# Cross attention on one core: three rotating units of two PSUM banks, one side bank, and a new order of the side work

## The reference, cut to what matters

```python
q = _split_heads(queries @ w_q.T + b_q)          # queries: layernorm(x); 16 heads of 16
k = _split_heads(keys @ w_k.T + b_k)             # keys, values: the context, 4096 rows
v = _split_heads(values @ w_v.T + b_v)
scores = einsum('bhqd,bhkd->bhqk', q, k) / sqrt(16)
weights = softmax(scores, axis=-1)
out = merge(einsum('bhqk,bhkd->bhqd', weights, v)) @ w_o.T + b_o
x = x + out
```

## Time and profile before

| of the profiled execution | |
|---|---|
| first cross attention (L862 to the last L134) | 0 to 1048 us |
| its first max matmul, its first scores | 40.0 and 80.5 us |
| second cross attention | 2961 to 3996 us |
| busy in 100 to 950 us: PE, DVE, ACT | 92%, 75%, 66% |
| granted PE clock in 100 to 950 us | 0.99 of full speed |
| busy DMA engines in the same stretch | 57% |

### The profile page before, as it was taken

One profiled execution on the slowest core, in us unless ns is written; L12 is line 12 of the kernel. 1 busy time (PEld: TensorE's weight loads), 2 busy tenths in 40 slices (PEclk: granted clock), 3 DMA queues, 4 the chain that ended last, 5 costly groups with the idle time before them and its releaser, 6 DMA issues. The chain is left out here.

```text
span 4469.0 us, 83297 instructions
## 1 busy us (share of the span) xinstructions
PE 4072.7 (91%) x30320; PEld 2916.0 (65%) x30320; DVE 3121.6 (70%) x7923; ACT 2814.7 (63%) x5769; POOL 1809.5 (40%) x1862
## 2 busy tenths in 40 slices
PE   6899999898979999999999999968999999977898
PEld 4555555555757888888878888845555555545677
DVE  5677777776777767667677676546777777767645
ACT  3666666667976777777677676715666666654322
POOL 3322222212566565555556555413223222201544
PEclk8999999999989999999999999989999999988999
DMA  6655556545020100001100101036556555512265
GB/s 153 133 105 108 103 98 115 109 64 203 10 76 5 34 31 30 24 29 32 39 22 25 38 22 38 15 84 138 114 101 111 102 106 106 100 27 70 83 177 190
DMA packets 208206, 354.14 MB, mean 79 GB/s; under 512 B 26927, under 2 KB 110564, under 8 KB 205745
## 3 DMA queue, kind: packets, MB, share of 16 engines
q1 hardware_dynamic: 200217, 338.42, 34.0%
q0 software_dynamic: 7584, 10.39, 0.7%
HBM read 257.48 MB, written 114.98 MB: 83 GB/s over the span
## 5 line engine op out<-in xcount | busy, mean ns | idle before, releaser
L754 DVE TENSOR_REDUCE xa_m_part<-xa_ring 128x1 f32<-128x512 f32 x2048 | 1318.4, 685 | 501.6 <-PE xa_ring L907 487.1
L676 ACT ACTIVATE xa_ex<-xa_sc 128x1024 f32<-128x1024 f32 x1024 | 991.4, 1022 | 120.6 <-PE xa_sc L893 105.4
L907 PE MATMUL xa_ring<-xa_ks,xa_q_base 48*128 48x512 f32 x2048 | 521.4, 500 | 166.9 <-DVE xa_m_part L754 131.6
L921 PE MATMUL xa_pv<-xa_ex,xa_vs 128*17 128x256 f32 x8192 | 553.1, 388 | 1.7 <-issue 1.7
L1068 POOL TENSOR_SCALAR lt_p<-lt_p,lt_stat 128x192 f32<-128x192 f32 x384 | 354.6, 924 | 456.0 <-DVE lt_stat L1058 455.4
L907 PEld LDWEIGHTS xa_ring<-xa_ks,xa_q_base 48*128 48x128 f32 x2048 | 202.6, 186 | 497.5 <-DVE xa_m_part L754 431.0
L1911 PE MATMUL lt_bank<-lt_wp,lt_xt 128*128 128x512 f32 x1728 | 465.6, 411 | 13.6 <-DVE lt_wp L1748 6.0
L893 PE MATMUL xa_sc<-xa_q_base,xa_ks 50*128 50x256 f32 x4096 | 423.7, 302 | 27.9 <-ACT xa_k L648 4.5
L893 PEld LDWEIGHTS xa_sc<-xa_q_base,xa_ks 50*128 50x128 f32 x4096 | 347.7, 188 | 122.3 <-ACT xa_vs L663 24.6
L1078 ACT ACTIVATE lt_p<-lt_p,lt_stat 128x128 f32<-128x128 f32 (+1 forms) x768 | 321.8, 420 | 157.4 <-DVE lt_stat L1053 154.8
L1911 PEld LDWEIGHTS lt_bank<-lt_wp,lt_xt 128*128 128x128 f32 x1728 | 315.2, 192 | 78.7 <-DVE lt_xt L1741 9.1
(11 more groups left out here) (325 smaller groups left out, 7943.0 us busy)
## 6 DMA issues: line engine op xcount, KB each, us to landing
xa_ks<-keys SPq DMA_DIRECT2D x372, 256.0 KB
keys<-xa_kp SPq DMA_DIRECT2D x128, 512.0 KB, 3.8
xa_cx<-in_ctx_t SPq DMA_DIRECT2D x64, 512.0 KB
lt_u<-in_lt_wqkv SPq DMA_DIRECT2D x54, 256.0 KB
places<-in_moe_blank SPq DMA_DIRECT2D x47, 258.0 KB, 9.6
moe_xs<-places SPq DMA_DIRECT2D x47, 258.0 KB
lt_w<-in_lt_w SPq DMA_DIRECT2D x6, 1536.0 KB
xa_q_base<-xa_m_rows SPq DMA_DIRECT2D x512, 2.0 KB
```

The costliest lines, as they stand in the source:

```text
L676: act.activation(x.ex[:, n % x.NE, :, :], x.sc[n % 2][:, :, :], ACT.Exp).then_inc(*x.ex_done.one())
L754: dve.tensor_reduce(x.m_part[:, i % 2, qt, h, ch:ch + 1], x.bank(n + odd), AX.X, ALU.max).then_inc(*x.dve_out.one())
L907: pe.matmul(x.bank(n + odd), x.q_base[rows, pair, b * S + qt * P:b * S + (qt + 1) * P], x.ks[unit % x.NU][rows, pair % 4, ch * 512:(ch + 1 ...
L921: mm = pe.matmul(x.pv[32 * j:32 * j + x.VW, :], x.vs[:, i % x.NV, kt, 4 * g + j, :], x.ex[:, n % x.NE, 2 * (j % 2) + j // 2, :], start=(kt ...
```

## The change

It touches `Cross` alone, in both stages.

- Banks: seven banks are dealt out anew. `units` are three tensors of two banks each, `pv` is one bank and `side` one. Max and scores of successive slots take turns in the three units: scores, max, scores, max, each the next unit. A step waits until the step three before it has been reduced (DVE) or exponentiated (ACT).
- Side work goes to `side` once weighing has begun, and to `side` and `pv` in turn before that. A `gather` that stands right behind a `max_rows` uses the other half of the same bank, with one common wait on ACT.
- The two heads of a max are reduced by one DVE instruction of 128 x (2 x 512), with one semaphore increment, in place of two of 128 x 512.
- The order in a step of two slots is now: scores, max, weigh, weigh, scores, max, then side work. `max_rows` and `gather` come together at the start of each quad (`gather` half a quad later than before).
- A key, value or query comes in each step whose side place is free (two in each step of the lead). `may_fill` holds back values until their buffer is free. In an item that gives side work in eight steps, `max_rows` with `gather` in four, and none in four. turn_out and project_out now take such places too, four slots later than before.
- The queries of batches 1 to 3, and their `stack_q`, move from slots 10 to 42 into the lead. `stack_k` is requested at slots 0 and 16 of an item, two slots earlier; that of unit 1 stands apart.
- `combine` is cut into three parts (L784; L786; the rest), in three successive steps.
- A memset of `xa_pv` (L716) goes.

```diff
-            self.ring = [ps(f"ring{i}", [P, 512]) for i in range(self.NW)]
-            self.pv = ps("pv", [P, S])
-            self.sc = [ps(f"sc{i}", [P, 4, S]) for i in range(2)]
+            self.units = [ps(f"unit{i}", [P, 2, 512]) for i in range(self.UNITS)]
+            self.pv, self.side = ps("pv", [P, 512]), ps("side", [P, 512])
...
+        queries = lambda b: [("query", b, mt) for mt in range(2)]
+        first = values(0)
+        out = self.keys(0, 1) + first[0:2] + queries(1) + first[2:4] + queries(2) + queries(3)
...
-        jobs = iter(self.filling())
-        for t in range(-self.LEAD, total + 20, 2):
+        jobs = self.filling()
+        outputs = [(batch * (b + 1) + at, (kind, b)) for b in range(B)
+                   for at, kind in ((18, "turn_out"), (22, "project_out"))]
+        for t in range(-self.LEAD, total + 24, 2):
             top = t + self.LEAD
             quad, at = divmod(t, 8)
             side = []
             if at == 0 and 0 <= quad + 1 < 4 * self.ITEMS:
                 side.append(("max_rows", quad + 1))
-            if at == 4 and 1 <= quad <= 4 * self.ITEMS:
-                side.append(("gather", quad - 1))
-            if t < 0 or at % 4 == 0:
-                job = next(jobs, None)
-                if job is not None:
-                    side.append(job)
-                    if job[0] == "value" and job[2] % 2 == 1:
-                        m = 2 * (job[1] + 1) + job[2] // 2
-                        if m < 2 * self.ITEMS:
-                            side.append(("split", m))
-                        if m + 2 < 2 * self.ITEMS:
-                            side.append(("ctx", m + 2))
-            b, at_b = divmod(t - 10, 12)
-            if 0 <= b < B - 1 and at_b in (0, 4):
-                side.append(("query", b + 1, at_b // 4))
-            if 0 <= b < B - 1 and at_b == 8:
-                side.append(("stack_q", b + 1))
-            b, at_b = divmod(t - batch, batch)
-            if 0 <= b < B:
-                if at_b == 14:
-                    side.append(("turn_out", b))
-                if at_b == 18:
-                    side.append(("project_out", b))
-            scores = [("scores", n) for n in (t, t + 1) if 0 <= n < total]
-            first, second = ([("max", top)], [("max", top + 1)]) if top < total else ([], [])
-            out += first + side + second + scores if side else first + scores + second
-            if second and top % 8 == 6:
+            if at == 0 and 0 <= quad - 2 < 4 * self.ITEMS:
+                side.append(("gather", quad - 2))
+            if not side and outputs and outputs[0][0] <= t:
+                side.append(outputs.pop(0)[1])
+            while len(side) < (2 if t < 0 else 1) and jobs and self.may_fill(jobs[0], t):
+                side.append(jobs.pop(0))
+            for odd in range(2):
+                if 0 <= t + odd < total:
+                    out.append(("scores", t + odd))
+                if top < total:
+                    out.append(("max", top + odd))
+                if odd == 0:
+                    out += [("weigh", n) for n in (t - 2, t - 1) if 0 <= n < total]
+            if top < total and top % 8 == 6:
                 out.append(("place_max", top // 8))
-            for n in (t - 2, t - 1):
-                if 0 <= n < total:
-                    out.append(("weigh", n))
-            unit, at_u = divmod(t + 30, 16)
-            if at_u == 0 and 1 <= unit < 2 * self.ITEMS:
+            for step in side:
+                out.append(step)
+                if step[0] == "value" and step[2] % 2 == 1:
+                    m = 2 * (step[1] + 1) + step[2] // 2
+                    out += [("split", m)] if m < 2 * self.ITEMS else []
+                    out += [("ctx", m + 2)] if m + 2 < 2 * self.ITEMS else []
+                if step[0] == "query" and step[2] == 1:
+                    out.append(("stack_q", step[1]))
+            unit, at_u = divmod(t + 32, 16)
+            if at_u == 0 and 2 <= unit < 2 * self.ITEMS:
                 out.append(("stack_k", unit))
-            if quad >= 2 and at == 2:
+            if t == 2 - self.LEAD:
+                out.append(("stack_k", 1))
+            if quad >= 2 and at >= 2:
                 b, kb = divmod((quad - 2) // 4, self.NKB)
                 if kb == self.NKB - 1 and b < B:
-                    out.append(("combine", b, (quad - 2) % 4))
+                    out.append(("combine", b, (quad - 2) % 4, at // 2 - 1))
+        assert not jobs and not outputs
...
+    def may_fill(self, job, t):
+
+        return job[0] != "value" or t > self.SLOTS * (job[1] - self.NV + 1)
...
+        first = [("side", self.side)] + [(f"{n}", self.units[2][:, n, :]) for n in range(2)]
         for step in self.plan:
             kind = step[0]
             started = started or kind == "max"
-            if kind == "scores":
-                buf = step[1] % 2
-                done[buf] = step[1] + 1
-                self.cleared[step[1]] = [last[2 * buf + i] for i in range(2) if 2 * buf + i in last]
             if kind in ("key", "query"):
                 self.chunk[step] = len(self.chunk)
-            if kind not in ("key", "value", "query", "max", "gather", "max_rows", "turn_out", "project_out"):
+            if kind in ("max", "scores"):
+                n = unit % self.UNITS
+                names, place = [f"{2 * n - 4}", f"{2 * n - 3}"], self.units[n]
+                unit += 1
+            elif kind in ("key", "query") and not started:
+                name, place = first[early % 3]
+                names, early = [name], early + 1
+            elif kind in ("key", "value", "query") and not weighed:
+                names, place = (["side"], self.side) if side % 2 else (["pv"], self.pv)
+                side += 1
+            elif kind in ("key", "value", "query", "max_rows", "turn_out", "project_out"):
+                names, place = ["side"], self.side
+            elif kind == "gather":
+                names, place = ["side"], self.side[:, S:2 * S]
+                if last[0] == "max_rows":
+                    self.beside[last] = step
+            elif kind == "weigh" and not weighed:
+                weighed, self.before[step] = True, [done["pv"]]
                 continue
-            self.use[step] = len(self.away)
-            engine = "dve" if kind in ("max", "project_out") else "act"
-            for _ in range(2 if kind == "max" else 1):
-                if kind == "max" or not started:
-                    at, bank = 4 + ring % self.NW, self.ring[ring % self.NW][:, :]
-                    ring += 1
-                else:
-                    at = side % 4 if not done[0] else 2 + (kind not in ("key", "value"))
-                    bank = self.banks[at]
-                    self.exps[step] = done[at // 2]
-                    side += 1
+            else:
+                continue
+            if kind != "scores":
+                engine = "dve" if kind in ("max", "project_out") else "act"
                 count[engine] += 1
-                self.bank_of.append(bank)
-                self.away.append((self.dve_out if engine == "dve" else self.act_out, count[engine]))
-                self.before.append(last.get(at))
-                last[at] = self.away[-1]
-
-    def bank(self, n):
-        return self.bank_of[n]
+                self.away[step] = (self.dve_out if engine == "dve" else self.act_out, count[engine])
+                self.use[step] = len(self.use)
+            else:
+                self.away[step] = (self.ex_done, step[1] + 1)
+            self.place_of[step] = place
+            beside = kind == "gather" and last[0] == "max_rows"
+            self.before[step] = [] if beside else [done[n] for n in names if n in done]
+            last = step
+            for n in names:
+                done[n] = self.away[step]
...
-                for odd in range(2):
-                    on.wait_ge(x.full, n + odd + 1)
-                    h = 2 * pair + odd
-                    dve.tensor_reduce(x.m_part[:, i % 2, qt, h, ch:ch + 1], x.bank(n + odd), AX.X,
-                                      ALU.max).then_inc(*x.dve_out.one())
+                on.wait_ge(x.full, n + 1)
+                dve.tensor_reduce(x.m_part[:, i % 2, qt, 2 * pair:2 * pair + 2, ch:ch + 1],
+                                  x.place_of[step][:, :, :], AX.X, ALU.max).then_inc(*x.dve_out.one())
...
+                on.wait_ge(x.xt_dve, NT // 4)
+                on.wait_ge(x.xt_act, NT // 4)
                 on.wait_ge(x.q_in[b], 12)
                 on.wait_ge(x.ks_in[unit % x.NU], 6 * (unit // x.NU + 1))
                 if ch:
                     on.wait_ge(x.rest_in, 6)
                 for odd in range(2):
                     rows = slice(64 * odd, 64 * odd + x.ROWS)
-                    pe.matmul(x.bank(n + odd),
-                              x.q_base[rows, pair, b * S + qt * P:b * S + (qt + 1) * P],
```

(29 more changed lines are left out.)

89 lines of the change are left out of this document (28 added, 61 removed).

## The result

The changed kernel took **4359.8 us** (median of 4 runs, 4357.6 to 4362.5); the kernel before, beside it, took 4459.4 (4455.1 to 4465.2). The ratio is 0.977, with an interval of 0.976 to 0.979: 99.6 us less, where 54 were forecast. The sign and the range were right, the size was half.

What follows compares the result with a forecast made beforehand. PE was taken as the bound, with only its waits to win. Per stage -8 - 18 - 2 + 1 = -27, so -54 for two stages from a median of 4458: 4405 us, own range 4375 to 4430, whole range 4340 to 4500.

Steps and rivals of the forecast that it cites:

- The new chain: Steps without side work: the next first max waits for the second scores' exponential, 2.96 us against 2.43 of PE work.
- The steps with `max_rows` and `gather`: Four steps of an item: PE 2.87 us, but the `xa_pv` copy adds about 0.13 to the chain, 3.09.
- The steps with a key or value: Eight of 16 steps in an item: the chain is covered by side work, PE takes 2.53 + 1.55 = 4.08 us.
- The steady pace: Quads of the steady part: 14.2 us against 14.37, a gain of 0.17 for some 50 quads, -8 us a stage.
- Batch ends: Three batch ends inside a stage's loop: excess falls from 10 to 4 us each, -18 us a stage.
- The lead: Start of a stage: lead grows by 15 us, excess of 20 in early quads falls to about 3; sum -2 us.
- The wide reduction: DVE reduction of 1024 elements from PSUM: 1.19 us, and the 0.18 us saved per slot saves no time.
- The end of a stage: Last part of a stage: same chain, with gather and the last combines a little later, +1 us.
- A: Rival, light steps: the chain is shorter or overlaps, so they cost only PE's 2.43 us; 4315 us, chance 0.10.
- B: Rival, changes between scores and max: each costs PE at most 0.1 us, +100 in all; 4505 us, chance 0.20.
- C: Rival, lead: the jam at the start costs +25 us more than forecast in both stages; 4455 us, no change, chance 0.15.
- D: Rival, steady part: 14.5 us per quad as an ACT copy takes the 0.2 margin, +30; 4435 us, chance 0.15.

Runs made afterwards that it cites:

- Weighs apart: The changed kernel with the two weighs of a step apart only in steps without side work; 4301.4 us, ratio 0.970.
- the kernel that missed: The changed kernel with weighs apart only in steps without side work, late queries one per item, one side job per lead step; 4344.5 us, ratio 0.980.

## Why the prediction was right, and where it was off

- **The new chain: right.** Light steps 3.04 where 2.96 was worked out; the 0.08 are the 0.54 from scores to exponential (485.36 to 485.90) that were put at 0.45. The wait names ACT, as said. Weighs apart took most of it away (41.2 to 13.3), and the steps fell to 2.63. The "0.35 + 0.45 us" of waiting in 7.25 that stands near the start of the prediction should be 0.37 + 0.35 by its own readings; nothing else was built on it.
- **The steps with `max_rows` and `gather`: right in size**, 3.04 for 3.09, but by two errors that cancel, which is luck. The 0.13 for the copy of `xa_pv` did not appear: the scores of 482.31 have their exponential at 482.86, 0.55 later, as without a copy. The same link had been put 0.09 too short.
- **The steps with a key or value: mis-sized**, 3.92 for 4.08. Scores (0.34) and the two weighs (0.99) are as forecast. The two maxima are not: they were priced at 0.43 each ahead of a weigh or a key, from a row that had itself just waited 0.37 for DVE. In the new kernel it is 0.32 for a max that is not held up (500.24 to 500.56, 501.89 to 502.21), and 0.43 for one that is let go late (486.98 to 487.41). But the wait is not the whole reason. The max of 387.39 did not wait and costs 0.43 all the same, and 0.43 is also the median of the 64 of its kind from 400 to 900 us of the kernel before (a max right behind a weigh and ahead of `max_rows` or `gather`). What differs is when the weights of the max are loaded (PEld is that part of PE). First the kernel before, then after:

```profile
387.39 0.19 PEld L907 LDWEIGHTS xa_ring<-xa_ks,xa_q_base 48*128 48x128 f32 x2 [0.42 <-DVE xa_m_part L754]
```

```profile
500.13 0.19 PEld L907 LDWEIGHTS xa_unit<-xa_ks,xa_q_base 48*128 48x128 f32 x2
```

  Behind a weigh or a key the load starts with the max itself (387.39 and 387.39); so it does for a max that is let go late. Behind scores it starts 0.11 ahead of it (500.13 and 500.24), while the scores still run. The old order put nearly every max that wasn't held up behind a weigh or side work, the new one puts every max of a step with scores behind them. So the new order gained about 0.1 us on each such max, for which the prediction had no term. That this is so because of the load is read from the rows; no experiment moved the max alone. Twice 0.11 for each of eight steps is 1.8 us to an item; the side piece, 1.61 for 1.55, takes 0.5 of it back.
- **The steady pace**, by these: 14.45 - 13.90 = 0.55 for each of 50 quads, 27 us, where 0.17 and 8 us were forecast. Of the difference of 0.38, 0.30 is the pace after, 13.90 for 14.2, which is the item of 55.7 for 56.8 and so mainly the maxima above; 0.08 is the pace before, read from three quads where 50 have a little more. It had been named the weakest term, as the small remainder of two large numbers, and the forecast's own range (4375 to 4430) was too narrow for it.
- **Batch ends: right in kind, a little low.** The excess fell from 9.6 to 2.0 on the average of the first stage's three, not from 10 to 4. The cut of the combine alone took 5.4 of it in the kernel before.
- **The lead: right.** +19.3 in each stage for +15, by the jam that was named. The first scores are at 92.83 (95 were forecast), and their exponential only at 99.35, behind two copies of keys on ACT. The rows of the jam in after, on POOL, PE and SP:

```profile
83.16 0.40 POOL L606 CAST xa_kp<-xa_k 128x256 fp32r<-128x256 f32 x1 [9.45 <-DMA keys<-xa_kp]
```

```profile
85.19 2.93 PE L863 MATMUL xa_pv<-xa_cxp,xa_wp 128*128 128x512 f32 x6 [5.79 <-ACT xa_k L655]
```

```profile
71.92 5.47 SPq L548 DMA_DIRECT2D xa_q_base<-keys  x12
```

  POOL waits for a buffer that a DMA to `keys` holds, ACT for POOL, and PE for ACT. With the queries elsewhere, the lead is 18 us shorter.
- **The wide reduction: right.** 1224 ns for 1.19 us, and no time in it.
- **The end of a stage: right in the second stage**, +1.1 (92.9 to 94.0) for +1, **and off in the first**, -4.5. There the trace of before has one quad of 17.2 where the second stage has 12.1: a max at 983.19 stood 3.48 us behind nothing that the profile shows, far from any combine. The trace of before has another such wait (2.28 at 3185.34, in a quad of 17.9), and so has the kernel before with the combine in parts, in other places. The 63 quads of the changed kernel have none over 1 us. The cause is open; by these quads some 9 of the 100 us are such waits, for which the forecast had no term.
- **The rivals.** A (PE-bound) gave 4315. The time lies halfway between it and the forecast, yet its mechanism is not seen: light steps have 3.04, not 2.43. B (a price for each change of kind) did not appear: scores to max is 0.34 wherever the max is not held up, and a max behind scores is the cheaper one. It has a core of truth elsewhere, in the single weigh (0.55 against 0.99 for two). C stayed at a lead of 19. D's lost margin did not occur in the changed kernel, but in the experiment with one weigh behind each max it did.

That the time came out at twice the forecast gain has thus no single reason: the steady pace gave 19 us more than forecast in the first stage, the batch ends and the end of the stage 5 each, and the lead took 4 back.

What stays open: whether the queries later add to the weighs apart by more than the few us that the intervals leave, and what each of the two edits to the lead did in the kernel that missed.
